# A two-layer graph network: the second layer's table filled in pieces of one row instead of eight

## The reference

```python
def layer(h, W, b, act):
    fwd_neigh = _seg_mean(h[src], dst, deg_in, n)
    bwd_neigh = _seg_mean(h[dst], src, deg_out, n)
    return act(jnp.concatenate([h, fwd_neigh, bwd_neigh], axis=1) @ W + b)

h = jnp.maximum(_layernorm(x), 0.0)
x = x + layer(layer(h, W1, b1, relu), W2, b2, identity)
h = jnp.maximum(_layernorm(x), 0.0)
agg = jax.ops.segment_sum(edge_attr, dst, num_segments=100000)
z = leaky_relu(jnp.concatenate([h, agg, u[batch]], axis=1) @ w1 + b1)
x = x + leaky_relu(z @ w2 + b2) @ w3 + b3
```

## Time and profile before

| | |
|---|---|
| median of 3 runs | 4495.09 us (4494.81 to 4498.89) |
| profiled execution | 4494.09 us |
| its span, first to last instruction | 4492.1 us |
| granted TensorE clock, mean | 0.930 |
| busy: PE, DVE, ACT, POOL | 3762.5, 3118.5, 2194.1, 3306.0 us |
| DMA packets, bytes | 898744, 767.65 MB |
| of these under 2 KB | 735203 |
| share of the 16 DMA engines: q1, q0 | 43.5%, 27.8% |

### The profile page before, as it was taken

One profiled execution on the slowest core, in us unless ns is written; L12 is line 12 of the kernel. 1 busy time (PEld: TensorE's weight loads), 2 busy tenths in 40 slices (PEclk: granted clock), 3 DMA queues, 4 the chain that ended last, 5 costly groups with the idle time before them and its releaser, 6 DMA issues.

```text
span 4492.1 us, 96303 instructions
## 1 busy us (share of the span) xinstructions
PE 3762.5 (84%) x24326; PEld 3234.2 (72%) x24326; DVE 3118.5 (69%) x10906; ACT 2194.1 (49%) x5395; POOL 3306.0 (74%) x3155
## 2 busy tenths in 40 slices
PE   8999877777777757666767677679999999999999
PEld 5666566666666656666666666668888888888888
DVE  8999876776777752322222222279999999999998
ACT  6777633333333322222222222257777777777776
POOL 6666488888888877888888888756666666666665
PEclk9999999999989988888888888889999999999999
DMA  7889766666666657888888888866666666666664
GB/s 231 257 250 259 214 163 163 163 163 163 163 161 162 162 128 190 204 204 198 204 204 194 204 204 198 194 124 135 136 132 135 135 133 135 133 134 136 133 135 101
DMA packets 898744, 767.65 MB, mean 171 GB/s; under 512 B 193759, under 2 KB 735203, under 8 KB 898707
## 3 DMA queue, kind: packets, MB, share of 16 engines
q1 hardware_dynamic: 657234, 600.12, 43.5%
q0 software_dynamic: 241472, 167.10, 27.8%
HBM read 457.42 MB, written 309.52 MB: 171 GB/s over the span
## 4 chain that ended last, share of the span: by engine, by line
PE 38%; DMA 9%; POOL 6%; issue 5%; DVE 2%; SPq 1%; ACT 1%; DVEq 0%; ACTq 0%; POOLq 0%
PE bank L1360 8%; DMA keyall<-keyrow 5%; PE bank L1375 4%; PE bank L1373 4%; PE bank L1374 4%; DMA ends<-pre,index 4%; POOL node L561 3%; POOL ends L546 3%; PE bank L1333 2%; PE bank L1337 2%; PE bank L1334 2%; PE bank L1338 2%; PE bank L1335 2%; PE bank L1347 2%; PE bank L1349 2%
## 5 line engine op out<-in xcount | busy, mean ns | idle before, releaser
L525 POOL DMA_INDIRECT pre<-summed,rep_index x392 | 641.2, 1636 | 154.1 <-issue 115.9
L561 POOL DMA_INDIRECT node<-summed,rep_index x392 | 623.9, 1592 | 132.4 <-issue 112.8
L592 POOL TENSOR_TENSOR resid<-node_out,b3s 128x128 f32<-128x128 f32 x784 | 336.8, 460 | 486.4 <-DVE rows L1109 482.4
L760 ACT ACTIVATE small<-bank,bias_small 128x512 f32<-128x512 f32 x784 | 533.9, 681 | 109.6 <-PE bank L1338 62.4
L1021 DVE TENSOR_SCALAR same<-keyall,keys 128x512 f32<-128x512 f32 (+3 forms) x392 | 138.0, 413 | 645.8 <-DMA keyall<-keyrow 645.8
L1169 PE MATMUL bank<-upper,table 112*128 112x256 bf16 x2744 | 403.6, 318 | 202.2 <-DVE upper L912 196.1
L1062 DVE SCALAR_TENSOR_TENSOR z<-bank,bias,small 128x512 f32<-128x512 f32 x784 | 548.9, 740 | 13.2 <-ACT small L760 8.1
L1169 PEld LDWEIGHTS bank<-upper,table 112*128 112x128 bf16 x2744 | 303.2, 113 | 291.1 <-DVE upper L912 214.2
L602 POOL TENSOR_TENSOR z_lo<-z,z_hi 128x512 fp32r<-128x512 f32 x392 | 494.8, 1280 | 13.9 <-ACT z_hi L792 13.9
L715 ACT ACTIVATE endsT<-bank,b1col 128x512 f32<-128x512 f32 x98 | 67.3, 687 | 839.3 <-PE bank L1250 839.3
L546 POOL DMA_INDIRECT ends<-pre,index x392 | 381.7, 974 | 124.2 <-issue 112.1
(11 more groups left out here) (137 smaller groups left out, 9778.3 us busy)
## 6 DMA issues: line engine op xcount, KB each, us to landing
node<-blank SPq DMA_DIRECT2D x98, 768.0 KB
node_out<-node SPq DMA_DIRECT2D x196, 384.0 KB, 3.5
rows<-in_x_dram SPq DMA_DIRECT2D x196, 256.0 KB
pre<-node_out SPq DMA_DIRECT2D x196, 256.0 KB, 3.2
keyall<-keyrow SPq DMA_DIRECT2D x196, 256.0 KB, 5.2
rows<-pre SPq DMA_DIRECT2D x196, 256.0 KB, 4.5
normed<-in_x_dram SPq DMA_DIRECT2D x196, 256.0 KB, 5.3
y<-node_out SPq DMA_DIRECT2D x196, 256.0 KB
```

What stands on the lines that cost most here:

```text
L525: pool.indirect_dma_start(pre1, bass.IndirectOffsetOnAxis(ap=rep_index[:, b, s:s + 1], axis=0), summed[:, b, s, 0:F], None, compute_op=ALU ...
L561: pool.indirect_dma_start(node1, bass.IndirectOffsetOnAxis(ap=rep_index[:, b, s:s + 1], axis=0), summed[:, b, s, :], None, compute_op=ALU. ...
L760: act.activation(small[:, m, :], bank[first_bank + m][:], ACT.Identity, scale=SLOPE, bias=bias_small[:, m:m + 1]).then_inc(ready, 1)
```

## The change

In the two fills the memory side is read as "(r p) f -> p r f" instead of "(p r) f -> p r f". Before, partition p wrote rows 8p to 8p + 7 of the fill's 1024, which are neighbours in memory. After, it writes rows p, 128 + p, 256 + p and so on: eight single rows, each 128 rows from the next. The tile, the bytes, the number of DMAs, their place in the order and their semaphore stay. As all rows of `blank` are equal, the table holds the same.

```diff
-                    sp.dma_start(node1[bass.ds(g * FILL, FILL), :].rearrange("(p r) f -> p r f", p=P), blank[:])\
+                    sp.dma_start(node1[bass.ds(g * FILL, FILL), :].rearrange("(r p) f -> p r f", p=P), blank[:])\
                         .then_inc(s_filled, 16)
...
-                sp.dma_start(node1[G * FILL:NR, :].rearrange("(p r) f -> p r f", p=P), blank[:, 0:GS // P, :])\
+                sp.dma_start(node1[G * FILL:NR, :].rearrange("(r p) f -> p r f", p=P), blank[:, 0:GS // P, :])\
                     .then_inc(s_filled, 16)
```

## The result

The changed kernel takes 4504.37 us (median of 20 runs, 4496.42 to 4507.32); the kernel before, in 20 runs beside it, 4495.97 us. The ratio, an estimate from all of these runs, is 1.0015, 95% interval 1.0008 to 1.0022: +6.7 us, between 3.6 and 9.9 (the two medians alone lie 8.4 us apart). The forecast was +4.7 us and "the same". The number held; the reason given for it did not.

The account below looks back on a forecast made before the run. POOL's issuing of indirect DMAs was taken to bound the first layer. The profiled 4494.1 us plus 4.7 us of passed waits gave 4498.8, or 4499.8 us beside the median (+0.1%, "the same"), range 4481 to 4516 us.

Parts of the forecast that it names:

- The bound: First layer: POOL issuing six indirect DMAs per group bounds it, not transfers; only 13.0 us are real waits.
- Packets: First layer's 98 fills: 1024 pieces of 768 B each instead of 128 of 6144 B, 88192 more packets in all.
- The price of 0.47 us per fill: DMA engines, first layer: 896 more packets at 8.47 ns over 16 engines add 0.47 us to a fill's 2.20 us.
- SyncE: Fill's issue in the first layer: 0.2 us more per group, hidden by SyncE's waits for DVE, so costed at nothing.
- part three: First layer, who waits behind the fill: later gathered rows delay DVE, then POOL's scatter; 4.7 us, between 0 and 19.4.
- the 41 waits: DVE's waits for gathered source rows in the first layer, 139.0 us; each grows by 0.47 us, 19.4 us in all.
- The 4.5 us of slack: First layer: copy done at 1201.82 us, its scatter begun at 1206.28; taken as slack that absorbs the delay.
- the count of 10: Groups 6 to 95: of 33 DVE waits over 1 us, 10 have the scatter within 1.1 us of the copy; 4.7 us.
- Rival 3: First layer: the gather gets past the fill's smaller pieces, landing up to 2 us earlier; at best 4482 us; chance 0.17.
- The common uncertainty: First layer: POOL's instructions lengthen beside DVE's work, 84 us in all; a tenth's shift moves the time 8 us either way.
- Rival 1: First layer, scatter's wait for the copy: all 41 waits pass their 0.47 us to POOL; 19.4 us, 4514.5 us; chance 0.16.
- rival 2: First layer's fills: dear pieces, 6.6 us per fill, 4564 us; milder, half rate from the 98304 B pitch, 22 to 90 us; chance 0.07.

Follow-up runs that it names:

- the shortened match: Kernel before, DVE's upper-digit match cut to one operation on 8 columns from the third group on, degrees replaced by ones: 4610.84 us, ratio 1.0246.
- a whole fill more: Kernel before, pieces of 6144 B kept, a second fill of the same size behind each, to an unread tensor: 4505.62 us, ratio 1.0027.
- the longer fill: Kernel before, pieces of 6144 B kept, a second DMA of 128 pieces of 1152 B behind each fill, to an unread tensor: 4496.35 us, ratio 0.9999.

## Why the prediction was right and wrong

- **The bound** was right: POOL issuing indirect DMAs, with few waits. The first table above shows it in its nine kernels; the shortened match is the one in which POOL waits much.
- **Packets**: 986936 forecast, 986935 in the page; q1's share 41.4% forecast, 41.0% measured. The price of 0.47 us per fill was 0.45 inside the layer and 0.59 alone. The formula gave 2.20 us for a fill that takes 1.88 alone; its stretches have other transfers beside the priced ones, which may be why, but no run shows it. The fixed overhead per packet of the Trainium skill ("DMA: Bandwidth & Descriptors", "Why small descriptors are slow") would give 11% on 1.88, an estimate of 0.2 us; the runs disagree, alone it is 31%.
- **SyncE** costs nothing, right; its instruction grew by 0.05 us and not by 0.2.
- **The step that failed is part three**, who waits behind the fill. I let each of the 41 waits grow by 0.47 us and passed 10 of them on to POOL. POOL's real waits did not grow from 13.0 to 17.7 us, they shrank to 4.0, and the added length alone is worth nothing in the run that isolates it. What I took as the order of things, a landing that is late by the fill's added length, holds in no run: in the meeting it is 1.4 us earlier with one row, 0.9 us earlier with a longer fill of the same pieces, and 0.3 us later with a whole fill more. The 4.5 us of slack was misread as well: that copy and scatter (1201.82 and 1206.28) come ahead of the end of DVE's wait at 1210.71. By the pairing that the count of 10 uses, the copy behind this wait ends at 1225.60 and its scatter starts at 1229.21, 3.6 us later.
- **Rival 3** (the gather gets past) had the right effect, by another mechanism, and the wrong time. The gather lands 1.4 us earlier, though it stands behind the fill as before, and POOL's real waits fell by 9.0 of the 13.0 us. I ended it there and asked nothing about what DVE does with its rows 1.4 us earlier.
- **The common uncertainty** was the cause. I had seen that gathers are longer beside DVE, and allowed a tenth of 84 us, 8 us, either way, as noise around the forecast. It moved by 28.8 us for the gathers and by 12.5 the other way for the scatters, and sets the sign. It should have stood as a case of its own.
- **Rival 1** (all waits pass) and **rival 2** (dear pieces) fell: the longer fill costs nothing; and pieces at a distance of 98304 B are written at 25.49 MB in 80 us, 319 GB/s, against 418 with eight rows, so neither the pitch nor the piece halves the rate (what each takes of the difference was not separated).
- So +4.7 against +6.7 us is agreement by chance: +28.8 and -12.5 us of longer and shorter instructions, for which my sum had nothing, and -10.2 us of idle time, for which it had +4.7, leave 6.1.

## What to carry to other kernels

When an engine is bound by its own instructions, ask what makes these longer before asking what it waits for: sum its busy and idle time in both kernels, term by term. A transfer that nobody waits for can still move the rhythm of two engines, by deciding when a neighbour's data land; try its place in the queue (here worth 12 to 14 us) before its shape. And test a cause by its parts, longer without finer and finer without longer: the sum of a prediction can be right with every term in it wrong.

## What the runs showed of the hardware

- A gather's instruction on POOL (128 rows) took 0.99 us beside none of DVE's matches, 1.02 us beside the digit match (f16 to bf16), 1.2 to 1.3 us beside the masking, and 1.9 to 2.0 us beside the key match (f32). Scatters went from 1.58 to 2.3 us beside the key match, up to 2.7. With the digit match shortened the key match did nothing to 115 scatters.
- Writes of 6144 B pieces from SBUF ran at 418 GB/s and of 768 B pieces at 319 GB/s, with next to nothing beside them.
- A gather of the software queue that was issued behind a fill of 768 KB started its packets 3.9 to 4.2 us (medians) after the fill's issue, whatever the size of the pieces from 6144 to 768 B; where no fill stood ahead of it, they started 0.7 to 0.8 us after its instruction's end. It landed 5.9 us after its instruction behind pieces of 6144 B and 4.3 to 4.4 us behind 3072 B or less. The Trainium skill ("DMA: Bandwidth & Descriptors", "Queues, rings and completion order") says that an engine changes between queues only after a whole packet, up to 64 descriptors. The trace agrees with an engine's share of a fill (8 to 64 pieces) that goes as a whole, and shows no gather that alternates with single pieces.
- One kernel showed two times 4% apart (4411.94 and 4616 to 4617 us) with unchanged code. What told them apart is open.
